# The second layer's steps in another order: gates in cycles 5, 6 and 9, the down product in cycle 12, spreads paired A with C and B with D

## The chip, the cores and the metric

One core of a Trainium2 chip runs the whole program. The metric is the device time of one launch in microseconds (us), the median of three runs. One more launch was profiled; every row below comes from it.

## The reference, cut to what matters

Eight batches of 512 tokens with 128 features go through two layers. Each layer is a layer norm and two branches that are added to the residual. Around the change:

```
# layer 0, for each of 8 batches: 16 channels in 8 pairs, rank 64
u, v = xn @ U.T * s, xn @ V.T * s
qh   = sigmoid(u_c @ v_c.T)                    # 512 x 512 a channel
G    = (qh @ v) @ U + (qh.T @ u) @ V           # "project"
x    = x + G * s + experts(xn)                 # experts: top-64 tokens each
# layer 1
k, q, v = elu1(xn @ Wk), elu1(xn @ Wq), xn @ Wv   # 64 features
for f in features:                             # 7 tiles of 128 features
    S_f = cumsum over time of (A_f k) * (B_f v)
    y  += top_f @ (S_f * C_f q) ; y += bot_f @ (S_f * D_f q)
x = x + (y / max(sum(z * q), 1e-6)) @ Wo + down(silu(gate(xn)) * up(xn))
```

The running sum replaces the reference's scan over time. A, B, C, D are constant matrices that spread 64 rows of k, v or q over the 128 features of a tile; the kernel calls these products spreads. Gate and up have 384 hidden units, three tiles of 128.

## The kernel before, in words

After a first part (routing, gather, experts, about 190 us) the kernel runs a loop over the batches. Pass i works on layer 0 of batch i and, in the same instruction stream, on layer 1 of batch i-1. Pass 0 has no second layer, passes 1 to 7 have both (a hardware loop, `iteration`, L1533), and a tail after them does layer 1 of batch 7 alone.

**Cycles.** A pass has 16 cycles (h = 0 to 15), two for each of 8 channel pairs. PE's order in a cycle is fixed: `scores` (L1429), four units of 128 rows, which fill the eight PSUM banks pairwise; then the cycle's middle, a list of steps from `middle_of` (L121, held in `MIDDLE`); then `weighted` (L1453), which multiplies the tanh of the scores; then perhaps a y round (`y_round`, L1483). ACT takes the tanh of the four units first (`tanh_unit`, L1106) and then its part of the middle. DVE does its part of the middle and then takes the accumulated output out of bank 6 (`evac_o`, L810, two operations on L818 and L820), which the fourth unit of the next cycle's scores needs free. The middle's steps get the banks 0, 1, 2, 3, 4, 5, 7 in order (`X_BANKS`), so each waits for the tanh of the unit that held its bank.

The middle of an even cycle always holds the steps pu, pv and pj (two projections of the next pair, one back), that of an odd one tu and tv (transposes). These belong to layer 0. The rest are layer 1's: back, norm, kq, v, the spreads, gate f and up f, down, den and yo.

**Spreads.** `ROWS_FIRST`, `ROWS_SECOND` (L70 to L73) list groups of spreads by cycle; `row_spread` (L1467) issues a group's matmuls in turns. A spread is two matmuls of 512 columns for tiles 0 and 1, and three for tiles 2 to 6 (high and low parts of fp32). A and B read partitions 0 to 63, C and D partitions 64 to 127, so that an A or B can run in the one half of the rows of the PE array while a C or D runs in the other. DVE multiplies A's bank with B's copy (made by ACT, L976 in the profile), scans the product over time (L869) and multiplies C's and D's banks with the scan (L875). C and D of a tile must come after its scan and before the next one's. Y round r needs tile r+1's D (round 0 takes C of tiles 0 and 1) and comes one cycle after it (`Y_AT`, L142).

**Feed-forward.** gate f and up f are three matmuls of 512 columns each (`product`, L1357). ACT takes the gate's tanh (L1138), DVE makes two multiplications (L892, L896). down is 12 fp32 matmuls, counted as 24 in the profile, and DVE adds the result to x (L899).

**The tail.** The same steps run in `TAIL_ORDER`, the groups of all cycles one after the other, with nothing beside them, over seven banks (`last_banks`, L219): step n waits until step n-7's bank is empty. Y rounds are put ahead of certain groups (L1549 on) and accumulate in one bank; ACT copies that bank before yo. den, yo and the add to x (L885) end it, and the store follows.

In the profile all matmuls of the helper `mm` stand on L1178. `sel_r` is the normed input of layer 1 or of layer 0, `kq_high` and `kq_low` hold k and q, `val_high` and `val_low` v, `e_high` and `e_low` the spreads' matrices, `arena` many buffers.

Of the kernel before, what the change touches and what calls it, by code (L numbers as in the profile page):

```python
# [40 lines left out]
B, T, D = 8, 512, 128  # L41
# [3 lines left out]
C, R = 16, 64  # L45
# [11 lines left out]
NF = 7  # L57
# [9 lines left out]

ROWS_FIRST = {4: (("B", 0), ("A", 0)), 5: (("A", 1),), 6: (("A", 2),), 7: (("D", 2), ("A", 3))}  # L70
ROWS_SECOND = {h: (("B", f + 1), ("C", f)) for h, f in ((4, 0), (5, 1), (6, 2), (7, 3), (9, 4), (11, 5))}
ROWS_SECOND |= {h: (("D", f), ("A", f + 1)) for h, f in ((8, 3), (10, 4), (12, 5))}
ROWS_SECOND[13] = (("C", NF - 1), ("D", NF - 1))  # L73
FULL_STEPS = {1: [("back", 0)], 2: [("norm", 0)], 3: [("kq", 0), ("v", 0)], 15: [("down", 0), ("den", 0), ("yo", 0)]}
FULL_STEPS |= {h: [("gate", f), ("up", f)] for h, f in ((9, 0), (11, 1), (13, 2))}

TAIL_ORDER = []
for _h in range(HALVES):
    TAIL_ORDER += [rows[_h] for rows in (ROWS_FIRST, ROWS_SECOND) if _h in rows]
    TAIL_ORDER += [(s,) for s in FULL_STEPS.get(_h, [])]  # L80
L1_STEPS = [s for group in TAIL_ORDER for s in group]
NL = len(L1_STEPS)
# [38 lines left out]
def middle_of(h):  # L121

    steps = FULL_STEPS.get(h, [])
    preps = [(kind, h // 2) for kind in PREP_IN_HALF[h % 2]] + [("sc", 0)] * (h == 1)
    work = []
    while steps or preps:
        work += steps[:1] + preps[:1]
        steps, preps = steps[1:], preps[1:]
    if ("norm", 0) in work:
        work = [w for w in work if w[0] != "norm"] + [("norm", 0)]  # L130
    return [("rows", rows[h]) for rows in (ROWS_FIRST, ROWS_SECOND) if h in rows] + work


def steps_of(work):
# [70 lines left out]
def build(nc, io):  # L205
    ctx = ExitStack()
    with ctx:
# [766 lines left out]
        def _(act):  # L974
# [168 lines left out]
            def iteration(i, attn, second):  # L1143
                if not attn:
                    for step in L1_STEPS:
                        l1(step, i - 1, last_banks[STEP_AT[step] % len(last_banks)])
                        if step == ("down", 0):
                            act.wait_ge(s_y, i * ROUNDS)
                            copy(y_sb[:], last_y_bank[:]).then_inc(s_ysb, 1)
                    return  # L1150
                for h in range(0 if second else FIRST_HALF, HALVES):
                    j = h // 2
                    g = i * PAIRS + j
                    q = g + 1
                    for u in range(TB):
                        tanh_unit(i, h * TB + u)
                    for work in MIDDLE[h] if second else FIRST_MIDDLE[h]:
                        if work[0] == "pu":
                            prep_raw(g, 1, u_raw, sums[:, 1], (j + 1) % 2, q, x_bank(work))
                        elif work[0] == "pv":  # L1160
                            prep_raw(g, 2, v_raw, sums[:, 0], (j + 1) % 2, q, x_bank(work))
                        elif work[0] == "tu":
                            prep_tok(g, 3, u_tok, (j + 1) % 2, q, x_bank(work))
                        elif work[0] == "tv":
                            prep_tok(g, 4, v_tok, (j + 1) % 2, q, x_bank(work))
                        elif not is_prep(work) and second:
                            for step in steps_of(work):
                                l1(step, i - 1, x_bank(step))
# [7 lines left out]
        def _(pe):  # L1176
# [289 lines left out]

            def row_spread(group, L, banks):  # L1467

                if ("A", 0) in group:
                    wait_emptied(pe, ("v", 0), L)  # L1470
                    pe.wait_ge(s_stk, L + 1)
                for n, (a, b) in enumerate(((0, 0), (0, 1), (1, 0))):
                    for (kind, f), bk in zip(group, banks):
                        last = 2 if f >= 2 else 1
                        if n <= last:
                            rows = slice(0, 64) if kind in "AB" else slice(64, 128)
                            at0 = (f + (NF if kind in "BC" else 0)) * P if a == 0 else (f - 2 + (NF - 2 if kind in "BC" else 0)) * P
                            ins = mm(bk[:], (e_high, e_low)[a][rows, at0:at0 + P], (val_parts if kind == "B" else kq_parts)[b][rows],
                                     n == 0, n == last)
                            if n == last:  # L1480
                                ins.then_inc(s_lf, 1)
# [51 lines left out]
            def iteration(i, attn, second):  # L1533
                L = i - 1
                if not attn:
                    wait_emptied(pe, ("yo", 0), L - 1)
                    project(i * PAIRS, 0, x_bank(("pj", 0)))
                    pe.wait_ge(s_prep_free, i * PAIRS * 4 + 4)

                    def tail_bank(step):  # L1540
                        n = STEP_AT[step]
                        if n >= len(last_banks):
                            wait_emptied(pe, L1_STEPS[n - len(last_banks)], L)
                        return last_banks[n % len(last_banks)]

                    def last_y_round(r):
                        y_round(r, L, last_y_bank, r == 0, r == ROUNDS - 1)

                    for group in TAIL_ORDER:  # L1549
                        kind, f = group[-1]  # L1550
                        if kind == "A" and f >= 3:
                            last_y_round(f - 3)
                        if kind == "D" and f == NF - 1:
                            last_y_round(ROUNDS - 2)
                        if kind == "den":
                            last_y_round(ROUNDS - 1)
                        if kind in "ABCD":
                            row_spread(group, L, [tail_bank(step) for step in group])
                        else:
                            if kind == "yo":  # L1560
                                pe.wait_ge(s_ysb, 1)
                            l1(group[0], L, tail_bank(group[0]))
                    return
                for h in range(0 if second else FIRST_HALF, HALVES):
                    j = h // 2
                    g = i * PAIRS + j
                    for u in range(TB):
                        scores(i, h * TB + u, second)
                    for work in MIDDLE[h] if second else FIRST_MIDDLE[h]:
                        kind = work[0]  # L1570
                        if kind == "sc":
                            wait_x_bank(work, h, i, second)
                            scatter(i, scatter_bank(i))
                        elif kind == "pj":
                            if isinstance(i, int) and i == 0 and j == 2:
                                pe.wait_ge(s_parts, 6)
                            wait_x_bank(work, h, i, second)
                            project(g, j, x_bank(work))
                        elif is_prep(work):
                            wait_x_bank(work, h, i, second)  # L1580
                            prep(g, PREP_K[kind], (j + 1) % PAIRS, i if j < PAIRS - 1 else i + 1, x_bank(work))
                        elif kind == "rows":
                            if second:
                                for step in work[1]:
                                    wait_x_bank(step, h, i, second)
                                row_spread(work[1], L, [x_bank(step) for step in work[1]])
                        elif second:
                            wait_x_bank(work, h, i, second)
                            if kind == "yo":
                                pe.wait_ge(s_yadd, L * ROUNDS + ROUNDS)  # L1590
                            l1(work, L, x_bank(work))
                    for un in range(h * TB, h * TB + TB):
                        weighted(i, un)
                    for r in range(ROUNDS):
                        if second and Y_AT[r] == h:
                            wait_x_bank(("y", r), h, i, second)
                            y_round(r, L, x_bank(("y", r)), True, True)
                if not second:
                    pe.wait_ge(s_pj_free, PAIRS - 1)
# [89 lines left out]
```

## Time and profile before

| what | value |
|---|---|
| median of 3 runs | 1527.62 us (1526.55 to 1527.67) |
| the profiled execution's own time | 1527.5 us |
| its span, first to last instruction | 1525.7 us |
| PE busy | 1465.7 us (96%) |
| DVE busy | 838.0 us (55%) |
| ACT busy | 746.3 us (49%) |
| mean granted clock of TensorE | 0.988 |
| pass 2 | 471.48 to 637.18, 165.70 us |
| its cycles 0 to 7 | 9.53, 9.89, 10.27, 8.98, 10.86, 8.72, 11.72, 8.92 us |
| its cycles 8 to 15 | 11.04, 10.56, 10.18, 10.59, 10.22, 11.26, 10.41, 12.55 us |

A cycle is counted from the first matmul of its scores to that of the next. Cycle 4, say, begins at 510.15 and cycle 5 at 521.01. The seven passes repeat each other within 0.1 us a cycle, but for the last cycle, which took 12.47 to 12.87 us. The time outside the span, 1.8 us, is launch and end.

### The profile page before, as it was taken

To read this page: it belongs to the slowest core of one execution; us is meant where nothing else is said; L and a number is where in the kernel's file an instruction comes from. 1 tells how busy PE (TensorE), PEld (TensorE's weight loads), DVE (VectorE), ACT (ScalarE), POOL (GpSimd) and SP (SyncE) were. 2 spreads that over 40 slices of the span, in tenths; PEclk is the share of its full clock that TensorE was granted. 3 is DMA by queue.
4 is the path that set the end of the run, shared out by engine and by line. 5 is a ranking of instruction groups with operands and counts; after the bars stand their busy time and mean duration, and the time that the engine had idled before them with its cause. 6 is when DMAs were issued, how large, how long until landed. Compare 5 with 4: busy or idle time off the path is not lost.

```text
span 1525.7 us, 25356 instructions
## 1 busy us (share of the span) xinstructions
PE 1465.7 (96%) x8470; PEld 872.7 (57%) x8470; DVE 838.0 (55%) x1521; ACT 746.3 (49%) x1170; POOL 44.5 (3%) x41
## 2 busy tenths in 40 slices
PE   6999699999999999999999999999999999999977
PEld 2676455556556556556565555555556556555644
DVE  8868633355554555555445554555545554555446
ACT  3336545555454545455545545455545544455521
POOL 4000400000000000000000000000000000000000
PEclk9999899999999999999999999999999999999988
DMA  6002100000000000000000000000000000000000
GB/s 201 1 14 71 37 1 1 0 8 1 1 1 10 8 1 1 10 8 1 1 2 16 1 1 1 10 8 1 1 10 8 1 1 1 10 1 1 1 7 8
DMA packets 24096, 17.91 MB, mean 12 GB/s; under 512 B 1632, under 2 KB 22240, under 8 KB 23936
## 3 DMA queue, kind: packets, MB, share of 16 engines
q1 hardware_dynamic: 23600, 14.27, 3.3%
q8 instruction: 85, 1.39, 0.4%
q0 software_dynamic: 336, 1.64, 0.3%
q14 instruction: 75, 0.61, 0.1%
HBM read 11.70 MB, written 4.19 MB: 10 GB/s over the span
## 4 chain that ended last, share of the span: by engine, by line
issue 86%; PE 8%; DVE 4%; ACT 1%; POOL 1%; DMA 1%; SPq 0%; DVEq 0%; POOLq 0%; ACTq 0%
PE psum L1178 7%; DVE arena L869 0%; DMA x_all<-in_x 0%; DVE upper L628 0%; DVE upper L644 0%; DVE upper L778 0%; DVE upper L776 0%; DVE upper L774 0%; DVE arena L875 0%; DVE upper L772 0%; DVE arena L867 0%; ACT upper L1090 0%; DMA expert_rows<-upper 0%; ACT upper L976 0%; DVE upper L785 0%
## 5 line engine op out<-in xcount | busy, mean ns | idle before, releaser
L1112 ACT ACTIVATE arena<-psum 128x1024 f32<-128x1024 f32 x504 | 475.7, 1030 | 606.3 <-PE psum L1178 597.1
L1178 PE MATMUL psum<-arena 128*64 128x512 f32 x2016 | 460.4, 598 | 2.3 <-ACT arena L1112 2.3
L1178 PEld LDWEIGHTS psum<-arena 128*64 128x64 f32 x2016 | 133.6, 136 | 251.1 <-issue 242.0
L1178 PE MATMUL psum<-v_parts,u_parts 64*128 64x512 f32 (+1 forms) x1568 | 204.5, 400 | 9.0 <-DVE o_hl L820 9.0
L818 DVE TENSOR_SCALAR o_hl<-psum,sums 128x512 fp32r<-128x512 f32 x126 | 94.5, 750 | 205.7 <-PE psum L1178 205.5
L1178 PE MATMUL psum<-u_parts,v_parts 64*128 64x512 f32 x1536 | 196.1, 399 | 4.3 <-issue 3.5
L1178 PEld LDWEIGHTS psum<-v_parts,u_parts 64*128 64x128 f32 (+1 forms) x1568 | 145.4, 185 | 91.2 <-issue 51.1
L1178 PEld LDWEIGHTS psum<-u_parts,v_parts 64*128 64x128 f32 x1536 | 139.4, 184 | 84.8 <-issue 54.4
L976 ACT ACTIVATE arena<-psum 128x512 f32<-128x512 f32 (+3 forms) x186 | 102.3, 606 | 65.5 <-PE psum L1178 47.4
L875 DVE TENSOR_TENSOR arena<-psum,arena 128x512 f32<-128x512 f32 x96 | 65.5, 690 | 123.8 <-PE psum L1178 119.7
L820 DVE SCALAR_TENSOR_TENSOR o_hl<-psum,sums,o_hl 128x512 fp32r<-128x512 f32 x126 | 94.6, 751 | 4.5
L1055 ACT ACTIVATE arena<-psum 128x512 f32<-128x512 f32 x128 | 76.5, 617 | 4.8 <-issue 2.7
L1408 PE MATMUL psum<-ident,arena 128*128 128x128 f32 x512 | 75.3, 278 | 2.1 <-ACT arena L1112 2.0
L737 DVE CAST u_parts<-arena 128x512 fp32r<-128x512 f32 x64 | 27.3, 427 | 82.3 <-ACT arena L1055 76.8
L1408 PEld LDWEIGHTS psum<-ident,arena 128*128 128x128 f32 x512 | 60.6, 143 | 18.9 <-ACT arena L1112 10.1
L869 DVE TENSOR_TENSOR_SCAN arena<-ones,arena 128x512 f32<-128x512 f32 x56 | 68.6, 1224 | 1.9
L1178 PE MATMUL psum<-sel_r,uT_hl 128*128 128x512 f32 x189 | 61.1, 431 | 1.2 <-ACT arena L1112 1.0
L1178 PE MATMUL psum<-o_hl,u_w_hl 128*128 128x512 f32 x189 | 54.0, 394 | 1.7 <-DVE o_hl L820 1.7
L1178 PE MATMUL psum<-sel_r,vT_hl 128*128 128x512 f32 x189 | 54.6, 397 | 0.0
L1178 PE MATMUL psum<-o_hl,v_w_hl 128*128 128x512 f32 x189 | 53.1, 389 | 0.0
L1178 PE MATMUL psum<-arena,top_w 128*64 128x512 f32 x96 | 50.4, 606 | 2.4 <-DVE arena L875 2.4
L1178 PE MATMUL psum<-arena,bot_w 128*64 128x512 f32 x96 | 50.4, 606 | 0.0
(214 smaller groups left out, 1604.5 us busy)
## 6 DMA issues: line engine op xcount, KB each, us to landing
x_all<-in_x SPq DMA_DIRECT2D x4, 512.0 KB, 6.1
upper<-in_we SPq DMA_DIRECT2D x8, 256.0 KB, 2.7
expert_rows<-upper SPq DMA_DIRECT2D x16, 128.0 KB, 2.5
xn_s<-expert_rows SPq DMA_DIRECT2D x8, 256.0 KB, 2.8
out<-x_all SPq DMA_DIRECT2D x8, 256.0 KB, 2.7
arena<-in_e POOLq DMA_DIRECT2D x1, 896.0 KB, 5.1
arena<-in_wi POOLq DMA_DIRECT2D x1, 576.0 KB, 5.5
uT_w<-in_uT SPq DMA_DIRECT2D x1, 512.0 KB, 6.3
```

What stands on the lines that cost most here:

```text
L737: link(nc.vector.tensor_copy(hl[:, par, 0], raw[:]))
L818: nc.vector.tensor_scalar(o_hl[:, o, 0], o_bank[:], total, None, ALU.add).then_inc(s_oh, 1)
L820: nc.vector.scalar_tensor_tensor(o_hl[:, o, 1], o_bank[:], total, o_hl[:, o, 0], ALU.add, ALU.subtract)\
L869: link(nc.vector.tensor_tensor_scan(pre[:], ones[:], ab[:], 0.0, ALU.mult, ALU.add))
L875: nc.vector.tensor_tensor(pc[half][:, r % 2], bk[:], pre[:], ALU.mult).then_inc(s_ld, 1)
L976: return nc.scalar.activation(dst, src, ACT.Copy)
L1055: nc.scalar.activation(raw[:], bk[:], ACT.Copy, accum_out=total[:, par:par + 1]).then_inc(s_prep_free, 1)
L1112: nc.scalar.activation(th_of(un), psum[:, at:at + 2], ACT.Tanh, scale=0.5 * FACTOR_SCALE ** 2).then_inc(s_th, 2)
L1178: return nc.tensor.matmul(out, lhsT, rhs, start=start, stop=stop)
L1408: ins = nc.tensor.transpose(bk[:, t * P:(t + 1) * P], (u_raw if k == 3 else v_raw)[:, t * P:(t + 1) * P], ident[:])
```

## The change

Three things: other groups of spreads, other cycles for gate, up and down, and with these another order of the tail. By cycle, layer 1's steps from cycle 4 on:

| cycle | before | after |
|---|---|---|
| 4 | B0 A0; B1 C0 | B0; A0 C0 |
| 5 | A1; B2 C1 | B1; A1 C1; gate 0, up 0 |
| 6 | A2; B3 C2; y0 | B2; gate 1, up 1; y0 |
| 7 | D2 A3; B4 C3 | A2 C2; B3 D2 |
| 8 | D3 A4; y1 | A3 C3; y1 |
| 9 | B5 C4; gate 0, up 0; y2 | B4 D3; gate 2, up 2 |
| 10 | D4 A5 | A4 C4; y2 |
| 11 | B6 C5; gate 1, up 1; y3 | B5 D4; A5 C5 |
| 12 | D5 A6 | B6 D5; down; y3 |
| 13 | C6 D6; gate 2, up 2; y4 | A6 C6; D6; y4 |
| 14 | y5 | y5 |
| 15 | down, den, yo | den, yo |

A semicolon parts groups. In the tail the y rounds now stand ahead of A3 (y0), A4, A5, A6 (y3), ahead of D6 (y4) and ahead of den (y5); before, y4 stood ahead of the group of C6 and D6.

```diff
--- before.py
+++ after.py
@@ -67,16 +67,16 @@
 
 
 
-ROWS_FIRST = {4: (("B", 0), ("A", 0)), 5: (("A", 1),), 6: (("A", 2),), 7: (("D", 2), ("A", 3))}
-ROWS_SECOND = {h: (("B", f + 1), ("C", f)) for h, f in ((4, 0), (5, 1), (6, 2), (7, 3), (9, 4), (11, 5))}
-ROWS_SECOND |= {h: (("D", f), ("A", f + 1)) for h, f in ((8, 3), (10, 4), (12, 5))}
-ROWS_SECOND[13] = (("C", NF - 1), ("D", NF - 1))
-FULL_STEPS = {1: [("back", 0)], 2: [("norm", 0)], 3: [("kq", 0), ("v", 0)], 15: [("down", 0), ("den", 0), ("yo", 0)]}
-FULL_STEPS |= {h: [("gate", f), ("up", f)] for h, f in ((9, 0), (11, 1), (13, 2))}
+ROWS = {4: [(("B", 0),), (("A", 0), ("C", 0))], 5: [(("B", 1),), (("A", 1), ("C", 1))], 6: [(("B", 2),)],
+        7: [(("A", 2), ("C", 2)), (("B", 3), ("D", 2))], 8: [(("A", 3), ("C", 3))], 9: [(("B", 4), ("D", 3))],
+        10: [(("A", 4), ("C", 4))], 11: [(("B", 5), ("D", 4)), (("A", 5), ("C", 5))], 12: [(("B", 6), ("D", 5))],
+        13: [(("A", 6), ("C", 6)), (("D", 6),)]}
+FULL_STEPS = {1: [("back", 0)], 2: [("norm", 0)], 3: [("kq", 0), ("v", 0)], 12: [("down", 0)], 15: [("den", 0), ("yo", 0)]}
+FULL_STEPS |= {h: [("gate", f), ("up", f)] for h, f in ((5, 0), (6, 1), (9, 2))}
 
 TAIL_ORDER = []
 for _h in range(HALVES):
-    TAIL_ORDER += [rows[_h] for rows in (ROWS_FIRST, ROWS_SECOND) if _h in rows]
+    TAIL_ORDER += ROWS.get(_h, [])
     TAIL_ORDER += [(s,) for s in FULL_STEPS.get(_h, [])]
 L1_STEPS = [s for group in TAIL_ORDER for s in group]
 NL = len(L1_STEPS)
@@ -128,7 +128,7 @@
         steps, preps = steps[1:], preps[1:]
     if ("norm", 0) in work:
         work = [w for w in work if w[0] != "norm"] + [("norm", 0)]
-    return [("rows", rows[h]) for rows in (ROWS_FIRST, ROWS_SECOND) if h in rows] + work
+    return [("rows", group) for group in ROWS.get(h, [])] + work
 
 
 def steps_of(work):
@@ -1144,7 +1144,7 @@
                 if not attn:
                     for step in L1_STEPS:
                         l1(step, i - 1, last_banks[STEP_AT[step] % len(last_banks)])
-                        if step == ("down", 0):
+                        if step == ("den", 0):
                             act.wait_ge(s_y, i * ROUNDS)
                             copy(y_sb[:], last_y_bank[:]).then_inc(s_ysb, 1)
                     return
@@ -1466,8 +1466,9 @@
 
             def row_spread(group, L, banks):
 
+                if ("B", 0) in group:
+                    wait_emptied(pe, ("v", 0), L)
                 if ("A", 0) in group:
-                    wait_emptied(pe, ("v", 0), L)
                     pe.wait_ge(s_stk, L + 1)
                 for n, (a, b) in enumerate(((0, 0), (0, 1), (1, 0))):
                     for (kind, f), bk in zip(group, banks):
@@ -1547,10 +1548,10 @@
                         y_round(r, L, last_y_bank, r == 0, r == ROUNDS - 1)
 
                     for group in TAIL_ORDER:
-                        kind, f = group[-1]
+                        kind, f = group[0]
                         if kind == "A" and f >= 3:
                             last_y_round(f - 3)
-                        if kind == "D" and f == NF - 1:
+                        if kind == "D":
                             last_y_round(ROUNDS - 2)
                         if kind == "den":
                             last_y_round(ROUNDS - 1)
```

## Rows read from the trace of the kernel before

**Rows 1.** Windows, core 0: us, busy per engine (instructions): PE, PEld, DVE, ACT, POOL; PEclk, DMA, GB/s

```profile
471.48:637.18 165.70, 165.20 (x976) 97.28 (x977) 88.67 (x150) 84.55 (x125) 1.01 (x1) 1.00 0.02 5
1489.00:1495.00 6.00, 5.50 (x20) 2.44 (x18) 4.80 (x7) 0.60 (x1) 0.00 (x0) 0.53 0.00 0
1495.00:1507.00 12.00, 10.50 (x56) 5.29 (x54) 11.59 (x17) 2.99 (x5) 0.00 (x0) 1.00 0.01 2
1507.00:1515.00 8.00, 6.93 (x16) 3.82 (x16) 4.19 (x7) 0.60 (x1) 0.00 (x0) 0.58 0.00 0
1485.45:1515.70 30.25, 26.48 (x103) 14.31 (x100) 24.70 (x32) 5.38 (x9) 0.00 (x0) 0.74 0.00 1
```

**Rows 2.** Timeline of PE in pass 2, cycles 12 and 13: start us, us, engine, line, operation

```profile
595.63 0.39 PE L1178 MATMUL psum<-kq_high,e_high 64*128 64x512 f32 x2
595.86 0.39 PE L1178 MATMUL psum<-kq_low,e_high 64*128 64x512 f32 x2
...
605.86 0.61 PE L1178 MATMUL psum<-kq_high,e_high 64*128 64x512 f32 x2
606.31 0.61 PE L1178 MATMUL psum<-kq_low,e_high 64*128 64x512 f32 x2
```

**Rows 3.** Timeline of PE in pass 2, cycles 7, 9, 10, 11 and 15

```profile
545.77 1.09 PE L1408 MATMUL psum<-ident,arena 128*128 128x128 f32 x8
546.79 3.65 PE L1178 MATMUL psum<-arena 128*64 128x512 f32 x16
...
565.05 0.97 PE L1178 MATMUL psum<-sel_r,gate_hl 128*128 128x512 f32 x3
567.53 3.65 PE L1178 MATMUL psum<-arena 128*64 128x512 f32 x16
...
571.97 3.01 PE L1178 MATMUL psum<-u_parts,v_parts 64*128 64x512 f32 x24
...
578.57 3.65 PE L1178 MATMUL psum<-arena 128*64 128x512 f32 x16
582.16 3.06 PE L1178 MATMUL psum<-v_parts,u_parts 64*128 64x512 f32 x24
...
627.59 2.94 PE L1178 MATMUL psum<-wd,hid 128*128 128x128 f32 x24
630.37 0.60 PE L1408 MATMUL psum<-ident,arena 128*128 128x128 f32 x4
```

**Rows 4.** Timeline of ACT in pass 2, cycle 7

```profile
542.61 3.77 ACT L1112 ACTIVATE arena<-psum 128x1024 f32<-128x1024 f32 x4 [5.80 <-PE psum L1178]
```

**Rows 5.** Timeline of PE in pass 2: first scores of cycles 2, 4 and 5

```profile
490.90 3.34 PE L1178 MATMUL psum<-u_parts,v_parts 64*128 64x512 f32 x24
...
510.15 3.02 PE L1178 MATMUL psum<-u_parts,v_parts 64*128 64x512 f32 x24
...
521.01 3.05 PE L1178 MATMUL psum<-v_parts,u_parts 64*128 64x512 f32 x24
```

**Rows 6.** Timeline of DVE in pass 2, behind cycles 1 and 4

```profile
492.47 0.75 DVE L820 SCALAR_TENSOR_TENSOR o_hl<-psum,sums,o_hl 128x512 fp32r<-128x512 f32 x1
...
521.13 0.75 DVE L818 TENSOR_SCALAR o_hl<-psum,sums 128x512 fp32r<-128x512 f32 x1
```

**Rows 7.** Timeline of DVE in the tail, its first, two late and its last operations

```profile
1485.45 0.69 DVE L867 TENSOR_TENSOR arena<-psum,arena 128x512 f32<-128x512 f32 x1 [2.10 <-ACT arena L976]
...
1511.61 1.29 DVE L875 TENSOR_TENSOR arena<-psum,arena 128x512 f32<-128x512 f32 x2 [2.36 <-PE psum L1178]
...
1518.78 0.69 DVE L899 TENSOR_TENSOR x_all<-psum,x_all 128x512 f32<-128x512 f32 x1 [3.10 <-PE psum L1178]
...
1521.84 1.13 DVE L885 SCALAR_TENSOR_TENSOR x_all<-psum,small,x_all 128x128 f32<-128x128 f32 x4 [0.69 <-PE psum L1178]
```

**Rows 8.** Timeline of PE in the tail, two waits

```profile
1507.44 0.64 PE L1178 MATMUL psum<-arena,top_w 128*64 128x512 f32 x1 [1.94 <-DVE arena L875]
...
1515.83 2.92 PE L1178 MATMUL psum<-wd,hid 128*128 128x128 f32 x24 [1.46 <-DVE hid L896]
```

## The prediction

> **What bounds the kernel now.** I read the windows first. In pass 2 PE is busy 165.20 of 165.70 us at the full clock, 1.00 of 2.4 GHz, DVE 88.67 and ACT 84.55 [rows 1]. So in the seven passes with both layers a change is worth what it takes from PE's stream. Then the timeline of PE, cycle by cycle, to see what a step costs and whether PE waits anywhere. Last the tail, where the picture is another: between 1485.45, where DVE begins the first A, and 1515.70, where it ends the last hidden tile, DVE is busy 24.70 of 30.25 us and PE gets a mean clock of 0.74 [rows 1]. There the order of steps counts, for DVE and PE wait for each other.
>
> **Spreads in the passes.** In cycle 12 D5 and A6 are issued in turns. Two matmuls, one in each half of the array's rows, start together, and the next two 0.23 us later. In cycle 13 C6 and D6 are in the same half: two matmuls take 0.45 us [rows 2]. So a pair of opposite halves costs one step of 0.228 us for two matmuls, and a cycle costs the larger of its two halves. Before, in steps: cycle 4: 6 (B0, A0 and B1, 2 each, with C0 beside them), cycle 5: 5, cycles 6 and 7: 6 each, cycles 8 to 12: 3 each, cycle 13: 6 (C6, D6). That is 44. After: 4, 4, 3, 6, 3, 3, 3, 6, 3 and 6 (A6 with C6, then D6 alone), that is 41. The gain is 3 steps, 3 x 0.228 = 0.68 us a pass.
>
> **Gates in the passes.** Their matmuls are the same. In cycle 9 gate, tu, up, tv take from 565.05 to 567.53, 2.48 us; tu and tv alone take 1.02 us in cycle 7 (545.77 to 546.79). A gate with its up costs 1.46 us [rows 3]. It is taken from 9, 11 and 13 and put into 5, 6 and 9. In 6 it stands among pu, pv and pj, six matmuls of 0.23 us, about 1.40. I count nothing for the difference.
>
> **Down and the y rounds.** Down costs 627.59 to 630.37, 2.78 us, and moves from cycle 15 to 12. A y round costs cycle 9's 4.44 us from the first weighted matmul to the next scores, less the 3.59 of cycle 10, so 0.85 us [rows 3]; y2 moves from 9 to 10 and y3 from 11 to 12. All at the same price in both places, so nothing in sum. No DMA is issued by a moved step, and nothing is moved past POOL. On SP the store of a batch waits for yo, which comes 2.78 us earlier against its cycle; no engine waits for that store in the passes.
>
> **What hides, and what it costs if the cover goes.** Three covers matter. (1) Weighted needs all four tanh. In cycle 7 these end at 546.38 (542.61 + 3.77), and PE reaches weighted at 546.79 [rows 3, 4]. A cycle emptier than 7 would gain nothing below that. Cycle 11 becomes like 7, and no odd cycle from 5 on becomes emptier. (2) The fourth unit of the scores waits for the evacuation of bank 6. Behind cycle 1 its second part ends at 493.22, 2.32 us after the scores of cycle 2 began (490.90), and these scores took 3.34 instead of 3.02 us: 0.32 lost [rows 5, 6]. Behind cycle 4 DVE evacuates at 521.13, directly behind its other work, 0.12 us after the scores of 521.01 [rows 5, 6]. Cycle 4 gets two steps shorter (0.46) and DVE's work there does not, since A0 still waits for ACT's copy of B0 behind four tanh. So the evacuation starts 0.58 us after the scores, and ends 2.11 after them. From the loss above, scores can take about 2.0; that costs 0.1 us a pass. (3) In cycle 5 DVE now has A1, its scan, C1, gate 0 and up 0: it may begin 5.5 us into the cycle (B1's copy) and ends at 9.6. The cycle becomes 8.72 - 0.23 + 1.46 = 9.95 us long, so the evacuation is due at about 10.0: covered by 0.4, and by 0.45 more before PE loses anything. In cycle 12 the same sum gives DVE 11 us of 13.9. Each us beyond would cost PE a us. Sum for the seven passes: 7 x (0.68 - 0.1) = 4.1 us; between 0 (the steps lost to such waits) and 7 x 0.76 = 5.3.
>
> **The tail.** Before, from 1485.45 to 1515.70: 24.70 us busy, the other 5.5 are four waits of 4.9 in sum and 0.7 of small gaps; the longest wait, 2.36, is ahead of C6 [rows 1, 7]. The cause of that one is PE, which waited 1.94 us with y4 for D5, and only then issued C6 and D6 [rows 8]. From 1515.70 to the end of the last add (1521.84 + 1.13 = 1522.97) another 7.3 us: down's 2.8 (PE from 1515.83, DVE's add waits 3.10), y5, den, yo [rows 7, 8]. After: down is done before A6, so 2.8 of the 7.3 go and 4.5 stay. DVE has the same 24.70 and its add of 0.69, plus 0.7 of small gaps: 26.1. It can begin 0.65 us earlier, as B0 now stands alone ahead of A0. New waits, followed step by step: PE must issue 26 single steps before A2 can be taken (B0, A0, B1, A1, gate 0, up 0, B2, gate 1, up 1, A2). At half clock, 0.53 in that stretch [rows 1], a step is 0.43, so 11.1 us, to 1494.5, where DVE would be ready at 1492.7: 1.8 us. A6 waits 0.4 behind down and y3. That gives 1484.8 + 26.1 + 2.2 + 4.5 = 1517.6, a gain of 5.4. The same working with the order of before ends at 1521.75, 1.2 us short of the trace, so like against like the gain is 4.2, and I take that. In sum 4.1 + 4.2 = 8.3 us.
>
> **The clock.** It stood at 0.53 in 1489 to 1495, though PE was 5.50 of 6 us busy, was 1.00 until 1507, and 0.58 after PE's wait of 1.94 us [rows 1, 8]. In the new order PE waits as long, 1.9 us, ahead of y5. If the clock falls there too, y5, den and yo cost up to twice as much: from down's end (1515.83 + 2.8) to the last add's start (1521.84) they take 3.2 us, 2.9 of them PE's [rows 7, 8], so up to 2.9 more. The Trainium skill says (TensorE: Matmul & The Clock Gate, Part 1: The HAM clock gate) that the throttled state is the default and that activity releases it. By that rule full-width gates early in the tail could raise the clock sooner, and the idle stretch ahead of y5 would lower it; the two rivals below price these from rows.
>
> **Rivals.** (a) The clock falls at the end of the tail: gain there 4.2 - 2.9 = 1.3, time 1527.5 - 5.4 = 1522.1; chance 0.17. For it speaks the equal wait, against it that down, behind a wait of 1.46 us, took 2.92 us, as in the passes (2.94) [rows 3, 8]. (b) The clock rises early in the tail: by hand, with every step at 0.228, the new order ends 1.9 us sooner, time 1517.3; chance 0.13. (c) The passes give nothing, since the new waits for evacuations eat the three steps (or the pairs A with C don't overlap as A with D do, which nothing suggests): 1527.5 - 4.2 = 1523.3; chance 0.08. (d) Slower: DVE's chain in cycle 5. If gate 0 and up 0 hold up the evacuation of bank 6 behind cycle 5, PE waits inside the scores of cycle 6. It decides from 0.85 us of delay on; to be slower over all by 3 us it needs (8.3 + 3) / 7 = 1.6 us of stall a pass, so 2.5 us of delay: time 1530.5. DVE's operations are too regular for that; chance 0.03.
>
> **The numbers.** Forecast: 1527.5 - 8.3 = 1519.2 for the profiled execution; that is 0.1 under the median of the runs, so 1519.3. Its chance is 0.59. The range reaches to 1514.5, with both terms at their upper end (5.3 in the passes, 5.4 + 1.9 in the tail gives 12.6), and to 1523.0, between (a) and (c). A measurement of this kernel tells 0.2%, 3 us, from no change. Faster by more than that, below 1524.6: 0.93; within: 0.04; slower: 0.03.
>
> **What would show it.** Right: passes of 165.0 to 165.1 us; cycles 12 and 15 of 13.8 and 9.8 us, 11 of 8.9; scores of cycle 5 about 0.1 us longer; the last add to x ending 4 us closer to the last pass. Wrong: a pass of 165.7 or more, with scores of 3.3 us behind cycles 4 or 5; two matmuls of a pair 0.45 us apart; PE at 0.5 of its clock in the last 4 us.

## The result, and the profile after

The changed kernel takes 1519.11 us (median of 4 runs, 1518.56 to 1519.62) against 1527.64 (1526.55 to 1530.20), a ratio of 0.9942 with a 95% interval of 0.9924 to 0.9959. The forecast was 1519.3. In a second set of runs (e11 below) it took 1518.97 us, ratio 0.9931 (0.9918 to 0.9945).

The profiled execution took 1518.56 us, its span is 1516.8 for 1525.7. From the page after (busy us, share, instructions), and the windows of pass 2 and of four stretches of the tail (columns as in rows 1):

```profile
span 1516.8 us, 25356 instructions
PE 1457.0 (96%) x8470; PEld 866.0 (57%) x8470; DVE 836.8 (55%) x1521; ACT 745.6 (49%) x1170; POOL 44.6 (3%) x41
```

```profile
470.69:635.96 165.27, 164.44 (x976) 96.53 (x977) 88.94 (x150) 84.48 (x125) 1.01 (x1) 1.00 0.02 5
1473.26:1478.87 5.61, 2.93 (x6) 1.82 (x7) 3.10 (x5) 1.15 (x2) 0.00 (x0) 0.50 0.00 0
1478.87:1485.30 6.43, 6.43 (x19) 4.30 (x19) 4.18 (x5) 1.79 (x3) 0.00 (x0) 0.52 0.00 0
1485.30:1508.00 22.70, 20.30 (x118) 11.48 (x118) 21.13 (x29) 4.18 (x7) 0.00 (x0) 1.00 0.01 1
1508.00:1514.02 6.02, 4.78 (x20) 3.68 (x20) 1.47 (x6) 0.60 (x1) 0.00 (x0) 0.58 0.00 0
```

Number and kind of instructions are the same; only their order changed. PE is as full as before in pass 2. The tail has another pattern of the clock than before: half until about 1485.1, full until 1509, half to the end. Before it was full at the first spread, fell 1 us behind it, and stood at half for 10.2 us while PE was busy 9.70 of them (the kernel before, same columns):

```profile
1483.41:1484.41 1.00, 1.00 (x6) 0.85 (x7) 0.00 (x0) 0.00 (x0) 0.00 (x0) 0.97 0.00 0
1484.41:1494.61 10.20, 9.70 (x34) 5.78 (x33) 7.86 (x10) 2.39 (x4) 0.00 (x0) 0.50 0.00 0
```

All of it comes back below.

**Where the time went.** Two marks split the 8.9 us of the spans: the first spread of the tail, and the end of the last add to x. The first stands at 1483.41 before and 1478.87 after (4.5 us), the second at 1522.97 and 1514.02 (8.95). So the passes gave 4.5 us and the tail 4.4: it took 39.56 us and now takes 35.15. A pass, as the mean of six, took 165.81 us and takes 165.17, 0.64 less; the last one with the head of the tail takes 0.75 less.

**The passes.** Cycles 4 to 14 of every pass now take 10.44, 9.95, 12.45, 8.92, 11.07, 9.70, 11.05, 8.92, 13.75, 9.79 and 10.37 us, each within 0.02 in all seven passes. Cycle 15 takes 9.75 to 10.42. The timeline of PE in pass 2 after, cycles 4 to 6 and 12, 13 and 15:

```profile
509.34 3.02 PE L1178 MATMUL psum<-u_parts,v_parts 64*128 64x512 f32 x24
519.78 3.02 PE L1178 MATMUL psum<-v_parts,u_parts 64*128 64x512 f32 x24
529.73 3.02 PE L1178 MATMUL psum<-u_parts,v_parts 64*128 64x512 f32 x24
...
591.85 3.04 PE L1178 MATMUL psum<-u_parts,v_parts 64*128 64x512 f32 x24
605.59 3.03 PE L1178 MATMUL psum<-v_parts,u_parts 64*128 64x512 f32 x24
...
625.75 3.03 PE L1178 MATMUL psum<-v_parts,u_parts 64*128 64x512 f32 x24
635.96 3.02 PE L1178 MATMUL psum<-u_parts,v_parts 64*128 64x512 f32 x24 [0.79 <-issue]
```

```profile
608.46 0.39 PE L1178 MATMUL psum<-kq_high,e_high 64*128 64x512 f32 x2
608.69 0.39 PE L1178 MATMUL psum<-kq_low,e_high 64*128 64x512 f32 x2
608.91 0.39 PE L1178 MATMUL psum<-kq_high,e_low 64*128 64x512 f32 x2
609.14 0.39 PE L1178 MATMUL psum<-kq_high,e_high 64*128 64x512 f32 x1
609.37 0.39 PE L1178 MATMUL psum<-kq_low,e_high 64*128 64x512 f32 x1
609.60 0.39 PE L1178 MATMUL psum<-kq_high,e_low 64*128 64x512 f32 x1
```

The second fence is cycle 13. A6 and C6 take three steps of 0.23 us for six matmuls, D6 alone three more. In [rows 2] two matmuls of C6 and D6 took 0.45. Scores take 3.02 us behind cycles 4 and 5: nothing waits for bank 6 there. Only those behind cycle 1 still take longer, 3.33 us.

**The tail.** DVE's waits, those of over 0.1 us, and its last operations:

```profile
1481.01 0.69 DVE L867 TENSOR_TENSOR arena<-psum,arena 128x512 f32<-128x512 f32 x1 [2.20 <-PE psum L1178]
...
1487.88 0.69 DVE L892 SCALAR_TENSOR_TENSOR arena<-arena,psum 128x512 f32<-128x512 f32 x1 [0.22 <-ACT arena L1138]
...
1504.67 0.69 DVE L867 TENSOR_TENSOR arena<-psum,arena 128x512 f32<-128x512 f32 x1 [0.60 <-PE psum L1178]
...
1510.90 0.16 DVE L878 TENSOR_SCALAR small<-psum 128x4 f32<-128x4 f32 x1 [2.97 <-PE psum L1178]
...
1512.89 1.13 DVE L885 SCALAR_TENSOR_TENSOR x_all<-psum,small,x_all 128x128 f32<-128x128 f32 x4 [1.61 <-PE psum L1178]
```

And PE's: down, the wait ahead of y5, den and yo.

```profile
1499.75 2.94 PE L1178 MATMUL psum<-wd,hid 128*128 128x128 f32 x24 [0.90 <-DVE arena L875]
...
1507.99 0.64 PE L1178 MATMUL psum<-arena,top_w 128*64 128x512 f32 x1 [1.50 <-DVE arena L875]
...
1509.00 1.86 PE L1178 MATMUL psum<-zsel,arena 128*128 128x1 f32 x8
1510.73 2.06 PE L1178 MATMUL psum<-wo,arena 128*128 128x128 f32 x8
```

From the first A to the end of the last D or hidden tile DVE took 1485.45 to 1515.70 before; now it takes 1481.01 to 1507.94, 26.9 us for 30.2, with down's add inside. The wait of 2.36 us ahead of C6 [rows 7] is gone. But den and yo run at half clock, where they ran at full clock before:

```profile
1519.68 1.05 PE L1178 MATMUL psum<-zsel,arena 128*128 128x1 f32 x8
1520.60 1.14 PE L1178 MATMUL psum<-wo,arena 128*128 128x128 f32 x8
```

### The profile page after: what moved, and what is told of

Read it like the earlier page. It is cut to its first block, busy times and chain, and to the rows that moved or that the text cites. A ratio compares the mean times of both kernels' runs of the same rounds, so it can differ in the third digit from the quotient of the medians.

```text
span 1516.8 us, 25356 instructions
## 1 busy us (share of the span) xinstructions
PE 1457.0 (96%) x8470; PEld 866.0 (57%) x8470; DVE 836.8 (55%) x1521; ACT 745.6 (49%) x1170; POOL 44.6 (3%) x41
## 4 chain that ended last, share of the span: by engine, by line
issue 86%; PE 7%; DVE 4%; ACT 1%; POOL 1%; DMA 1%; SPq 0%; DVEq 0%; POOLq 0%; ACTq 0%
PE psum L1178 7%; DVE upper L628 0%; DMA x_all<-in_x 0%; DVE arena L869 0%; DVE upper L644 0%; DVE upper L774 0%; DVE upper L778 0%; DVE upper L776 0%; DVE upper L772 0%; DVE arena L875 0%; DMA expert_rows<-upper 0%; DVE upper L771 0%; ACT upper L1090 0%; ACT upper L976 0%; DVE upper L785 0%
## 5 line engine op out<-in xcount | busy, mean ns | idle before, releaser
L976 ACT ACTIVATE arena<-psum 128x512 f32<-128x512 f32 (+3 forms) x186 | 105.4, 611 | 53.0 <-PE psum L1178 46.3
L875 DVE TENSOR_TENSOR arena<-psum,arena 128x512 f32<-128x512 f32 x96 | 64.6, 689 | 50.2 <-PE psum L1178 48.3
L867 DVE TENSOR_TENSOR arena<-psum,arena 128x512 f32<-128x512 f32 x32 | 22.1, 691 | 79.4 <-PE psum L1178 52.8
```

The lines of the kernel that those rows point to most:

```text
L867: nc.vector.tensor_tensor(ab[:], bk[:], bs_of(f)[:], ALU.mult).then_inc(s_ld, 1)
L875: nc.vector.tensor_tensor(pc[half][:, r % 2], bk[:], pre[:], ALU.mult).then_inc(s_ld, 1)
L976: return nc.scalar.activation(dst, src, ACT.Copy)
```

## The experiments

Below, "tail" is the time from the first spread to the end of the last add in the profiled execution of a run. "Cycles 0 to 14" and "cycle 15" are means over six passes of it. Before these are 39.56, 153.17 and 12.63; after 35.15, 155.09 and 10.08. The launches of one kernel spread: the changed kernel's nine lie in 3.5 us, and 23 launches of the kernel before in 8.4 (1523.81 to 1532.25). The start of pass 1 lies between 305.3 and 308.2 from one profile to the next. So the parts are read in the traces and the medians only confirm. A tail comes from one profile, too. After, e11, e6 and e7 have the same program there and took 35.15, 35.43, 34.77 and 35.61 us, so a difference of less than about 0.8 us between two tails tells nothing by itself.

### e1: the new groups of spreads, with late gates and down last

```diff
-FULL_STEPS = {..., 12: [("down", 0)], 15: [("den", 0), ("yo", 0)]}
-FULL_STEPS |= {h: [("gate", f), ("up", f)] for h, f in ((5, 0), (6, 1), (9, 2))}
+FULL_STEPS = {..., 15: [("down", 0), ("den", 0), ("yo", 0)]}
+FULL_STEPS |= {h: [("gate", f), ("up", f)] for h, f in ((9, 0), (12, 1), (13, 2))}
```

> The changed kernel with its new groups of spreads, but the gates late (cycles 9, 12 and 13) and down in cycle 15, as before. Theory 1 (what counts in the passes is steps of the busier half of the PE array, 41 for 44; gates and down cost the same anywhere): a pass of 165.1 to 165.2 us against 165.8 before, 4.5 us over seven passes, and cycle 13 among the longest. Rival (the passes gained because gates and down now fill cycles in which PE had to wait for tanh or evacuations): no gain in the passes, 165.7 or more. Tail: by hand 35 us from the first spread to the end of the last add, against 35.2 in the changed kernel and 39.6 before; if the early gates are what brings the clock up early, it comes up about 11 us after the first spread as before, not 6. Total by theory 1: 1519.3; by the rival: 1523.

1520.18 us, ratio 0.9954 (0.9939 to 0.9968). Cycles 0 to 14: 152.57, so 0.60 less than before; a pass 165.18. Tail 36.34. Theory 1 holds: the groups bring most of what the change brings. (One gate pair differs from before as well: gate 1 and up 1 stand in cycle 12, not in 11.) The early rise of the clock does not hang on the early gates either: here they are late, and the clock was full 5 us after the first spread all the same. Cycle 5, with four steps and nothing else, took 8.59 us where its matmuls sum to 8.49: that is the cover of the tanh.

DVE's rows of this tail, the first A, the last hidden tile and down's add:

```profile
1482.13 0.69 DVE L867 TENSOR_TENSOR arena<-psum,arena 128x512 f32<-128x512 f32 x1 [2.20 <-PE psum L1178]
...
1506.76 0.69 DVE L896 SCALAR_TENSOR_TENSOR hid<-arena,psum 128x512 f32<-128x512 f32 x1
1511.84 0.69 DVE L899 TENSOR_TENSOR x_all<-psum,x_all 128x512 f32<-128x512 f32 x1 [4.38 <-PE psum L1178]
```

Between the first two DVE has no wait of over 0.1 us: 25.3 us where the old order took 30.2, though gate 2 and up 2 still stand behind D6. So the wait of 2.36 us ahead of C6 goes with the groups, which put C6 beside A6 and ahead of y4.

### e2 and e12: the moves alone

```diff
 # e2, on the kernel before
-... 15: [("down", 0), ("den", 0), ("yo", 0)]} ... ((9, 0), (11, 1), (13, 2))}
+... 12: [("down", 0)], 15: [("den", 0), ("yo", 0)]} ... ((5, 0), (8, 1), (9, 2))}
 # e12, the same with
+... ((5, 0), (9, 1), (11, 2))}
```

In both, ACT's copy of the y bank moves from down to den, as in the change.

> The kernel before with its old groups of spreads, but gates in cycles 5, 8 and 9 and down in cycle 12. Theory 1: passes as before, 165.8 us (44 steps), cycle 12 about 2.7 longer, cycle 15 about 2.6 shorter, nothing in sum. Rival (the moves are the gain): passes of 165.1. Tail: down leaves the end, 35 to 36 us from the first spread to the end of the last add, against 39.6 before. Total by theory 1: 1523.3; by the rival: 1519.

> The kernel before with its old groups of spreads, gates in cycles 5, 9 and 11, down in cycle 12. The same moves with gates in 5, 8 and 9 left only three steps of spreads in cycle 11, which took 9.44 us where its matmuls summed to 9.12. Theory (a cycle whose middle is shorter than ACT's four tanh waits for them, so what is taken from it below that is not gained): with a gate in cycle 11 it takes 10.6 us as before and the pass 165.8, 0.4 less than with the gates in 5, 8 and 9; the tail 35 to 36 us from the first spread to the end of the last add; total 1524 to 1525, so the moves alone are worth 3 to 4 us, all in the tail. Rival (the moves disturb the passes elsewhere, say at the loop's end, where down left): pass 166.1 or more, total 1527.

e2: 1527.88 us, ratio 1.0003 (0.9994 to 1.0013): nothing gained. e12: 1527.00, ratio 0.9992 (0.9984 to 1.0001). The passes did not get faster in either, so the rival of e1 is out. But I had expected 1523 to 1525, from the tail, and that was wrong. The traces show three reasons.

First, e2's passes are slower. Cycle 11 takes 9.44 us; the timeline of PE there:

```profile
590.63 1.09 PE L1408 MATMUL psum<-ident,arena 128*128 128x128 f32 x8
591.96 3.65 PE L1178 MATMUL psum<-arena 128*64 128x512 f32 x16 [0.24 <-ACT arena L1112]
```

In cycle 7 before, these transposes and the weighted matmuls stood 1.02 us apart [rows 3]; here it is 1.33, and the wait is for the tanh. With a gate left in cycle 11 (e12) it takes 10.58 us as before, and cycles 0 to 14 take 155.87 for 156.16. So a middle shorter than ACT's tanh gives nothing back, and e12's expectation for that cycle came out. An e2 pass takes 166.25, 3.1 us more than before over seven.

Second, down's move costs a little: 12.91 - 10.22 = 2.69 in cycle 12, and cycle 15 gets back 12.63 - 10.12 = 2.51. e12's pass is 166.0. Over seven passes that is 1.3 us, which the expectation did not have (it is half of its rival). The difference is small beside what cycle 15 varies by, but all profiles agree: it takes 12.60 to 12.82 in the mean of the five kernels with down in it, 10.08 to 10.34 in that of the nine without.

Third, the tail: 35.42 in e2, but 37.03 in e12, whose yo ran at half clock (DVE waited 1.61 us for it, as in the profile after); that is 1.0 of the 1.6 between them. By these parts e2 should be about 1.0 us faster than before and e12 1.2; the intervals of the medians reach to 0.9 and 2.4 us faster.

### e3: down back in cycle 15

```diff
-FULL_STEPS = {..., 12: [("down", 0)], 15: [("den", 0), ("yo", 0)]}
+FULL_STEPS = {..., 15: [("down", 0), ("den", 0), ("yo", 0)]}
```

> The changed kernel with down put back to cycle 15; all else stays. Theory 1: passes the same within 0.1 us each. In the tail down (2.8 us of PE) stands again behind D6; if my count is right that the gain in the tail is down's leaving the end, it gets 2 to 2.8 us longer: 1521.5. Rival: down then fills PE's wait of 1.5 us ahead of y5 and keeps its clock up for y5, den and yo (1.7 us in the changed kernel's trace), and A6 no longer waits 0.6 us: the tail stays within 0.7 us, total 1519 to 1519.8, and what the tail gained comes from C6 and D6 no longer being issued behind y4's wait.

1518.24 us, ratio 0.9936 (0.9923 to 0.9949). Tail 35.47, only 0.3 more than with down moved and within what one tail program varies by; the rival holds. PE's row of down and DVE's last add:

```profile
1506.06 4.57 PE L1178 MATMUL psum<-wd,hid 128*128 128x128 f32 x24
```

```profile
1513.73 1.13 DVE L885 SCALAR_TENSOR_TENSOR x_all<-psum,small,x_all 128x128 f32<-128x128 f32 x4 [0.69 <-PE psum L1178]
```

Down ran mostly at half clock (4.57 for 2.94 us), yet it follows D6 without a wait: DVE multiplies C6 and D6 meanwhile, and y5 has nothing to wait for. den and yo then ran at full clock. So moving down away from the end is not worth the 2.8 us by which the end gets shorter. Cycles 0 to 14 took 152.43: three steps and the cheaper place of gate 1, 0.74 less than before.

### e7 and e6: how much DVE work cycle 5 can take

```diff
+        spare = sb("spare", [P, 8])
...
+                    if second and h == 5:
+                        for n in range(4):      # e6: range(1)
+                            nc.vector.tensor_reduce(spare[:, n:n + 1], ones[:], AX.X, ALU.max)
```

> The changed kernel with four more DVE operations of about 0.69 us in cycle 5, behind up 0 and ahead of the evacuation of bank 6 (they reduce a constant into a tile that nothing reads). DVE waits 0.62 us there in the changed kernel, and the evacuation ends 1.65 us after the next scores began where 2.0 is allowed. Theory (the cover of cycle 5 is about 1.0 us, and beyond it PE waits one for one inside the scores of cycle 6): 2.75 us more work costs 1.75 us a pass, scores of cycle 6 of 4.8 us for 3.0, total 1519.1 + 12 = 1531. Rival (evacuations are hidden however late): within 1 us of 1519.

> The changed kernel with one more DVE operation of 0.69 us in cycle 5 ahead of the evacuation of bank 6. Theory (cover of about 1.0 us: DVE's wait of 0.62 and 0.35 before the fourth unit needs the bank): no cost, 1519.1, scores of cycle 6 at 3.0 us. Rival (each operation of DVE ahead of the evacuation delays PE): 0.1 to 0.7 us a pass, 1520 to 1524.

e7: 1529.71 us, ratio to before 1.0014 (1.0003 to 1.0024): the whole gain is gone. e6: 1520.16, ratio 0.9950 (0.9937 to 0.9964), cycle 6 12.42 us, cycles 0 to 14 155.17: no cost in the passes. The timelines of e7 around the evacuation behind cycle 5, DVE and PE (lines are shifted by one to three):

```profile
530.34 2.46 DVE L955 TENSOR_REDUCE spare<-ones 128x1 f32<-128x512 f32 x4
532.72 0.74 DVE L819 TENSOR_SCALAR o_hl<-psum,sums 128x512 fp32r<-128x512 f32 x1
533.49 0.75 DVE L821 SCALAR_TENSOR_TENSOR o_hl<-psum,sums,o_hl 128x512 fp32r<-128x512 f32 x1
```

```profile
530.88 2.33 PE L1182 MATMUL psum<-u_parts,v_parts 64*128 64x512 f32 x18
534.38 0.97 PE L1182 MATMUL psum<-u_parts,v_parts 64*128 64x512 f32 x6 [1.17 <-DVE o_hl L821]
```

Eighteen of the 24 matmuls run, the last six wait for the evacuation. Cycle 6 takes 13.87 us, 1.42 more, in all passes: 7 x 1.42 = 9.9 us, against 10.6 measured. The four operations took 2.46 us, not 2.75, so the cover of cycle 5 is 2.46 - 1.42 = 1.0 us, as expected. This is rival (d) of the prediction made by hand: its mechanism and place are real, and the change stays 1 us clear of it.

### e11, e5, e4, e8: the clock in the tail

e11 is the changed kernel again. e5 puts matmuls that nothing reads where PE waits for DVE at the head of the tail, e4 puts five ahead of y5, e8 does both.

```diff
+                    def idle_work(n, bk):
+                        for _ in range(n):
+                            mm(bk[:], gu_hl[0][:, 0, 0:P], e_high[:, 0:512])
...
                         kind, f = group[0]
+                        idle_work({"back": 2, "norm": 14, "kq": 4, "B": 8}.get(kind, 0)
+                                  if f == 0 else 0, last_y_bank)                        # e5, e8
...
                         if kind == "den":
+                            idle_work(5, tail_bank(("yo", 0)))                          # e4, e8
                             last_y_round(ROUNDS - 1)
```

> The changed kernel once more, unchanged, beside the three below. If the clock's falls and rises in the tail follow from the program alone, it shows the same trace: half clock from 7 us ahead of the first spread to 6 us behind it and again from y5 on, 35.2 us from the first spread to the end of the last add. If their time is chance (as the spread of the other runs suggests: two kernels with the same tail up to there stood at the full clock at the first spread), it lies anywhere in 32.5 to 35.5. Total 1518.5 to 1519.7 in either case.

> The changed kernel with 28 matmuls of 512 columns at the head of the tail, where PE waits for DVE: 2 ahead of back, 14 ahead of norm, 4 ahead of kq and v, 8 ahead of B0; into the y rounds' bank, which y0 overwrites. Theory (the clock is at half from the first spread for want of work before it): kqv takes 1.6 for 2.93 us, spreads go at 0.23 a step from the start, DVE gets A0 about 0.7 sooner and no longer waits for gate 1: 1.3 to 2 us less, 1517.4. Rival 1 (DVE's chain sets the head anyway): within 0.5 us of 1519.1. Rival 2 (the clock is down already when the matmuls come, 0.43 us each, so that 14 of them take 6.0 us for a wait of 4.6): 1 to 3 us slower.

> The changed kernel with five matmuls of 512 columns in the tail, behind D6 and ahead of y5, into yo's bank, which yo overwrites; nothing reads them. PE waits 1.50 us there. Theory (the clock fell because PE waited; y5, den and yo then cost up to 1.7 us more): den takes 1.05 for 1.86 us and yo 1.14 for 2.06, the end comes 1.2 to 1.7 us sooner, 1517.6. Rival (the clock falls for the many short waits of the whole stretch, or at its own time): no gain, 1519.1, or up to 0.3 more if the matmuls overrun the wait.

> The changed kernel with both fillings: 28 matmuls that nothing reads at the head of the tail, and 5 ahead of y5. Theory (half clock in the tail is for want of work, and costs at both places): full clock from head to end, 32.4 to 33.2 us from the first spread to the end of the last add, total 2 to 2.7 below the changed kernel beside it. Rival (only the head counts, or nothing does beyond chance): within 0.5 us of the kernel with the filling at the head alone, 34.2 us of tail.

| run | median us | ratio to before | first spread at | den, yo | tail |
|---|---|---|---|---|---|
| e11, changed kernel | 1518.97 | 0.9931 (0.9918 to 0.9945) | half clock | 1.87, 2.05 | 35.43 |
| e5, filled at the head | 1516.07 | 0.9927 (0.9913 to 0.9940) | full | 1.80, 2.06 | 34.21 |
| e4, filled ahead of y5 | 1518.34 | 0.9934 (0.9921 to 0.9948) | full, then half from 1483.1 to 1486.5 | 1.05, 1.14 | 32.53 |
| e8, both | 1515.51 | 0.9910 (0.9895 to 0.9925) | full | 1.05, 1.14 | 32.55 |

e8 is the fastest kernel of the study, 3.5 us under the changed kernel of the same set (their intervals against before just overlap). In the traces: from the start of pass 7 to the first spread 180.82 us for 182.08, and the tail 32.55 for 35.43, 4.1 us in all, more than the 2 to 2.7 expected. e5 gives 2.4 us in the traces, 1.3 to 2 expected. In e4 den and yo took what theory said, but its median shows no gain: the ratio is nearly e11's. e8's end, PE and DVE:

```profile
1506.02 1.43 PE L1178 MATMUL psum<-e_high,gate_hl 128*128 128x512 f32 x5
1508.60 1.05 PE L1178 MATMUL psum<-zsel,arena 128*128 128x1 f32 x8
1509.51 1.14 PE L1178 MATMUL psum<-wo,arena 128*128 128x128 f32 x8
```

```profile
1480.80 0.69 DVE L867 TENSOR_TENSOR arena<-psum,arena 128x512 f32<-128x512 f32 x1 [1.52 <-ACT arena L976]
...
1509.69 0.16 DVE L878 TENSOR_SCALAR small<-psum 128x4 f32<-128x4 f32 x1 [2.15 <-PE psum L1178]
...
1510.75 1.13 DVE L885 SCALAR_TENSOR_TENSOR x_all<-psum,small,x_all 128x128 f32<-128x128 f32 x4 [0.69 <-PE psum L1178]
```

Where PE's waits are filled, the clock stays up, and each place has its price: 1.7 us at the end (e5 against e8), 1.2 at the head of the tail and 1.2 ahead of it (e11 against e5). The Trainium skill (TensorE: Matmul & The Clock Gate, Part 1: The HAM clock gate) says that activity releases a throttled default; e8 agrees, with a clock of 1.00 over its whole tail. The stretch of the kernel before from 1484.4 to 1494.6, at half with PE busy 9.70 of 10.20 us, does not follow from that sentence alone. e4's tail is as short as e8's by luck at its head: its program is e11's up to y5, and yet the clock was full again at its first spread, and the fall 1 us behind it, 3.4 us long, cost nothing that shows in the tail. e6, too, began its spreads at full clock. So where the falls lie in time varies from launch to launch. How much of the spread of the launches this makes is not shown.

### e9 and e10: the two orders with the clock mostly up

```diff
 # e9, on the kernel before: the same at its head, and
+                        if kind == "down":
+                            idle_work(5, tail_bank(group[0]))
                         if kind == "D" and f == NF - 1:
+                            idle_work(7, tail_bank(group[0]))
 # e10, on e3: the same at its head, and
+                        if kind == "A" and f == NF - 1:
+                            idle_work(5, tail_bank(group[0]))
...
                         if kind == "D":
+                            idle_work(4, tail_bank(group[0]))
```

> The kernel before with the same filling at the head of its tail, 7 matmuls ahead of y4 (where PE waits 1.94 us) and 5 ahead of down (1.46 us). It takes the clock out of the comparison of the two tails. Theory 1 (the order of the tail is worth what I worked out at the full clock for both, 35.4 against 32.2 us, so 3.2): 35.4 to 36.2 us from the first spread to the end of the last add for 39.6, total 1523.8. Rival (most of the tail's gain was the clock's): 33.5 us or less, total 1521.5.

> The changed kernel with down back in cycle 15, the filling at the head, 5 matmuls ahead of y3 and 4 ahead of y4, where PE waits 1.49 and 1.21 us. There down took 4.57 us at half clock. Theory (down at the end fills the wait for D6, so that it costs nothing but what it exceeds that wait, if the clock stays up): 32.8 us from the first spread to the end of the last add, level with the filled changed kernel, total 1516.5. Rival (down at the end is on the path in full at full clock): 1 us or more behind it.

e9: 1524.92 us, ratio 0.9979 (0.9970 to 0.9989), tail 37.27. e10: 1516.52, ratio 0.9920 (0.9907 to 0.9934), tail 33.49. So the old order took 37.27, the new one (e8) 32.55, and the new one with down last 33.49. e9 missed its 36.2 by 1.1: its clock still fell once, from 1493.3 to 1496.7, behind a wait of 3.1 us ahead of y0, and DVE waited 1.00 us for PE in that stretch. So 37.27 is too much for the old order at full clock; 36.3 would be my estimate, the one less the other. e10's clock fell too, from 1479.6 to 1483.0, but there DVE had no wait. e10 missed its 32.8 by 0.7 and lies nearer to its rival. DVE's waits in e9 ahead of C6, and the one for down that stays:

```profile
1512.48 1.29 DVE L875 TENSOR_TENSOR arena<-psum,arena 128x512 f32<-128x512 f32 x2 [0.95 <-PE psum L1178]
...
1518.97 0.69 DVE L899 TENSOR_TENSOR x_all<-psum,x_all 128x512 f32<-128x512 f32 x1 [3.10 <-PE psum L1178]
```

The order of the tail is worth 4.7 us filled, or 3.7 if that wait is taken off, and 4.4 unfilled. The clock took at least 2.3 us of the old tail and 2.6 to 2.9 of the new. Of the order's worth, down's place is 0.9 (e10 against e8). No run splits the rest with the clock up. Unfilled, the groups with late gates and down last (e1) take the tail from 39.56 to 36.34, the early gates with them (e3) to 35.47. But the moves with the old groups (e2) take it to 35.42 as well, so the parts do not add: the groups shorten the stretch from the first A to the last D or hidden tile (30.2 to 25.3 us in e1), the moves mostly the end behind it (7.3 to 4.4 in e2), and in the new order each has less left to take.

## Why the prediction was right

**Steps of spreads: right.** 44 to 41 steps, 0.68 us a pass forecast. Cycles 0 to 14 without down's 2.68 give 155.09 - 2.68 = 152.41, 0.76 less than before. The rest, 0.08, is for the most part gate 1 in cycle 6, 1.40 for 1.46, which I had seen and counted as nothing. e1 shows that the groups do it.

**Gates and y rounds: right. Down: not free.** Cycles 5, 11 and 12 came within 0.1 us of what the prices give: 9.95 for 9.95, 8.92 for 8.9, 13.75 for 13.8. But cycle 15 took 10.08 for 9.8. Down's move cost 2.68 us and brought back 2.55, where I had 2.78 both ways. That loss of 0.13 a pass was not in the sum.

**Covers.** (1) The tanh: right, and e2 shows the price where it is gone, 0.3 us a pass. (2) The evacuation behind cycle 4: I took 0.1 us a pass for it, and it was nothing. DVE's evacuation began 0.34 us after the scores and not 0.58, since its work in cycle 4 got 0.2 shorter. Its rows after:

```profile
520.12 0.74 DVE L818 TENSOR_SCALAR o_hl<-psum,sums 128x512 fp32r<-128x512 f32 x1
520.89 0.75 DVE L820 SCALAR_TENSOR_TENSOR o_hl<-psum,sums,o_hl 128x512 fp32r<-128x512 f32 x1
```

It ends at 521.64, 1.86 us after the scores of 519.78, inside the 2.0. (3) Cycle 5: 0.85 us of cover forecast, 1.0 measured (e7). A pass got 0.64 us shorter where 0.58 was forecast, the passes together gave 4.5 us for 4.1. That this is so close owes something to down's loss and the evacuation's 0.1 cancelling. (For the 0.76 in the upper bound of the range the prediction gives no working.)

**The tail: the size was right, 4.4 for 4.2, the working of it was not, and the agreement is luck.** From the first spread, the working had 1.4 us to the first A, 28.3 to the last D and 4.5 to the end, 34.2 in all. Measured were 2.1, 26.9 and 6.1, so 35.15.

The start: "It can begin 0.65 us earlier" did not come, since the new kernel stood at half clock at its first spread and the old one at full. In e8, at full clock, the first A comes 1.47 us behind it.

The middle: I had charged 1.8 us of waits ahead of A2. They did not come (0.22 was left, for gate 1's tanh), for the clock rose 6 us after the first spread. That was rival (b), with a chance of 0.13. The wait ahead of C6, whose cause I had named, did go, and e1 shows that the groups took it away.

The end: "Down is done before A6, so 2.8 of the 7.3 go and 4.5 stay" is right as a sum at full clock, for e8 has 4.35 there. As the cause of the gain it failed. With down put back (e3) the tail is 0.3 longer, and 0.9 where PE's waits are filled (e10): down last fills a wait of PE that is there otherwise, and its add leaves DVE's stretch ahead. And rival (a) came, with 0.17: den and yo at half clock, 1.7 us of the 2.9 that I had priced. PE at half clock in the last 4 us, which I had listed as a sign of being wrong, is what the trace shows.

So the errors are 0.75 too little, 1.4 too much and 1.6 too little. Their sum, about 1.0, is nearly the 1.2 that I had taken off because the same working came out 1.2 short for the old order. The allowance was not made for these errors. The chances for (a) and (b) were too low: e11, e7 and e6 end with den and yo at half clock as well, and e11, e1, e3 and e7 have the early rise.

**What stays open.** Why the clock rose 5.1 to 6.4 us behind the first spread in every profile of the new groups that began at half (after, e1, e3, e7, e11), and 9.7 to 11.2 us behind it in those of the old ones (e2 and e12, which began at half, and before, which fell 1 us behind it). No run was made that changes the first groups alone. Also open is why cycle 15, the loop's end, is the only one that varies, by up to 0.7 us.

## What to carry to other kernels

Where the matmuls use half of the array's rows, count steps of the busier half in each stretch between barriers, not matmuls: a regrouping with the same instructions is worth its steps, in every pass. Moving work between stretches of a full engine is worth nothing in itself, and costs where it empties a stretch below the chain that runs beside it. Where an engine order ends in a tail without cover, interleave what hangs on a long chain and put nothing behind a wait that could stand ahead of it (here C6 behind y4); and where PE must wait there, matmuls that nothing reads can pay, since they keep its clock.

## What the runs showed of the hardware that was not expected

- The granted clock stood at half from 1 to 11 us behind the first spread in the tail before, with PE busy 9.70 of these 10.20 us.
- The clock at one place of the same program differs between launches: half at the first spread after and in e11, full in e4 and e6, whose tail is the same up to there.
- 33 matmuls added to the tail made the kernel 3.5 us faster (e8 against e11, by the medians; 4.1 by the traces).
- Cycles 4 to 14 repeat within 0.02 us over the passes, cycles 0 to 3 within 0.1. The last took 12.47 to 12.87 before and 9.75 to 10.42 after, and PE's idle time at its end, 0.33 to 1.00 us in these two profiles, stands as issue, not as a wait for another engine.
